# Delaying the recurrence scan by one more head, squaring in place, and one temporary fewer in the quantiser, in an eight-core layer kernel

## The reference, cut to what matters

```
# recurrent branch, h = 32 heads, n = 128 states
delta = softplus(delta_bias[..., :, None] + B_ssm[..., None, :])
hst   = exp(d_t * A) * hst + d_t * d_t          # over 2048 steps
y     = einsum('blhn,bln->blh', hs, C_ssm)
s     = ((y[..., None] + xg * Dp) * sigmoid(xn @ Wg + bg)) @ Wo
# feed-forward branch, twice: quantise the activations, take the sign of the weights
x_q = clip(round(x_norm * scale), -128, 127) / scale
w_q = sign(w) * mean(abs(w))
h   = gelu(x_q @ w1_q.T + b1);  f = quant(h) @ w2_q.T + b2
```

## Time and profile before

| | us |
|---|---|
| device time of the runs of this kernel | 3325.84 and 3452.18, median 3389.01 |
| profiled execution | 3321.91 |
| its span, slowest core (core 5) | 3320.1 |
| spans of the eight cores | 3305.1 to 3320.1, granted TensorE clock 0.766 to 0.768 |
| VectorE busy | 1435.8 (43% of the span) |
| TensorE matmuls busy | 1668.6 (50%) |
| ScalarE busy | 928.3 (28%) |
| GpSimd busy | 620.7 (19%) |

### The profile page before, as it was taken

The page is one execution under the profiler, slowest core; times in us unless marked ns, Lnnn a source line. Parts: engine busy times, 40 slices in busy tenths (PEclk is TensorE's granted clock), DMA queues, the critical chain, the costliest instruction groups (busy, mean ns, idle before and its releaser), DMA issues.

```text
span 3320.1 us, 23086 instructions; the slowest of 8 cores (3305.1 to 3320.1 us)
## 1 busy us (share of the span) xinstructions
PE 1668.6 (50%) x6432; PEld 648.1 (20%) x6432; DVE 1435.8 (43%) x1415; ACT 928.3 (28%) x981; POOL 620.7 (19%) x264
## 2 busy tenths in 40 slices
PE   2221263434342383777777777760000039999942
PEld 1100120000000131333332332320000014444421
DVE  4566334444544131222222222228999913333355
ACT  3100025545453010000222222221111155464322
POOL 0000013333333000000333333324444400000000
PEclk9999975555555796888888888875555569999965
DMA  4100125555553506111222222223333364554244
GB/s 116 51 26 26 18 42 123 107 121 111 117 115 88 90 1 101 38 38 64 102 102 102 102 102 102 101 77 116 123 115 123 108 215 175 178 203 177 77 152 165
DMA packets 129723, 340.84 MB, mean 103 GB/s; under 512 B 17664, under 2 KB 68992, under 8 KB 114080
## 3 DMA queue, kind: packets, MB, share of 16 engines
q1 hardware_dynamic: 114144, 287.78, 24.8%
q0 software_dynamic: 15456, 51.58, 10.1%
HBM read 290.10 MB, written 100.66 MB: 118 GB/s over the span
## 4 chain that ended last, share of the span: by engine, by line
PE 42%; DVE 22%; issue 12%; ACT 8%; DMA 7%; POOL 4%; another core or an unknown queue 3%; DVEq 1%; SPq 0%; ACTq 0%; POOLq 0%
PE pmA L816 15%; PE pmA L1012 14%; DVE p_t L952 6%; PE pmA L731 4%; DMA p_s<-s1Tsc 4%; POOL p_u L626 3%; PE pmA L695 3%; DVE p_t L945 2%; DVE aw L608 2%; ACT p_dmp L603 2%; ACT p_w L612 2%; PE pmC L401 2%; ACT p_d L621 2%; DVE p_k L949 1%
## 5 line engine op out<-in xcount | busy, mean ns | idle before, releaser
L1012 PE MATMUL pmA<-p_k2g,p_s 128*128 128x512 bf16 x2048 | 460.9, 382 | 474.2 <-ACT p_s L1001 474.2
L816 PE MATMUL pmA<-k1T,p_s 128*128 128x512 bf16 x2048 | 484.2, 396 | 168.3 <-DMA p_s<-s1Tsc 168.3
L1012 PEld LDWEIGHTS pmA<-p_k2g,p_s 128*128 128x128 bf16 x2048 | 191.8, 98 | 744.3 <-issue 535.9
L841 POOL TENSOR_TENSOR p_acs<-p_acs,p_h 128x1024 f32<-128x1024 f32 x63 | 213.2, 3383 | 432.0 <-ACT p_h L831 432.0
L581 PE MATMUL pmA<-ehl,bsel_t 32*128 32x512 bf16 x256 | 108.7, 562 | 365.5 <-DVE p_d L588 354.9
L816 PEld LDWEIGHTS pmA<-k1T,p_s 128*128 128x128 bf16 x2048 | 199.1, 101 | 454.4 <-issue 259.0
L824 DVE TENSOR_TENSOR p_h<-pmA,p_a1b 128x512 f32<-128x512 f32 x128 | 88.5, 691 | 380.6 <-PE pmA L816 380.3
L1026 DVE TENSOR_TENSOR p_S<-p_S,pmA 128x1024 f32<-128x1024 f32 x112 | 136.7, 1221 | 260.6 <-PE pmA L1012 260.6
L548 DVE TENSOR_TENSOR_SCAN p_h<-p_a,p_u 128x2048 f32<-128x2048 f32 x32 | 141.6, 4424 | 236.5 <-POOL p_u L626 236.5
L939 POOL TENSOR_TENSOR p_v<-p_hg,p_c2b 128x1024 f32<-128x1024 f32 x64 | 177.4, 2773 | 263.2 <-ACT p_int L942 233.6
L827 ACT ACTIVATE p_hg<-p_h,p_b1c 128x512 f32<-128x512 f32 x128 | 92.4, 722 | 458.2 <-DVE p_h L824 458.2
(11 more groups left out here) (160 smaller groups left out, 1806.8 us busy)
## 6 DMA issues: line engine op xcount, KB each, us to landing
p_w<-w2T SPq DMA_DIRECT2D x64, 1024.0 KB, 5.1
p_w<-w1T POOLq DMA_DIRECT2D x64, 512.0 KB, 10.4
s1Tsc<-p_w SPq DMA_DIRECT2D x256, 128.0 KB, 7.2
p_s<-s1Tsc SPq DMA_DIRECT2D x16, 2048.0 KB, 8.7
hgsc<-p_hg SPq DMA_DIRECT2D x64, 512.0 KB, 2.6
p_hg<-hgsc SPq DMA_DIRECT2D x64, 512.0 KB, 3.5
p_xb<-x_sh SPq DMA_DIRECT2D x16, 1024.0 KB, 5.8
k2Tsc<-p_k SPq DMA_DIRECT2D x64, 256.0 KB, 2.1
```

What stands on the lines that cost most here:

```text
L816: bld.op(TE, lambda e, k=k, icl=icl, tc=tc, pb=pb, sb_=sb_: e.matmul(pb[:, 0:512], sb_[:, k * 512 + icl * 128:k * 512 + (icl + 1) * 128], ...
L841: bld.op(GP, lambda e, h2b=h2b: e.tensor_add(acs[:], acs[:], h2b[:]), reads=[(h2b, 0), (h2b, 1), (acs, 0)], writes=[(acs, 0)])
L1012: bld.op(TE, lambda e, ic=ic, ds=ds, tc=tc, pb=pb, kg=kg, s2b=s2b: e.matmul(pb[:, tc * 512:(tc + 1) * 512], s2b[:, ic * 2048 + ds * 128:ic ...
```

## The change

In the recurrence:

- The scan and its product with C (`tail_vg`) for head h-1 are no longer called in iteration h; both `tail_vg` and `tail_y` are now called for head h-2, one behind the other. The last two heads follow after the loop.
- The square is written over `p_d` itself, the tile `p_u` is gone, and the scan reads `p_d`. `p_d` and `p_a` have three buffers instead of two. Since ScalarE's L623 (exp) reads `p_d`, the square now waits for it, and no longer only for L621 (ln).
- ScalarE's absolute sum of an odd w1 tile is done in two halves of 1024 columns, each with its own column of `aw1`, which grows to 128 columns; a memset clears its second half and the final sum reads 128 columns. The scratch tile that takes the unused output shrinks from 2048 to 1024 columns.

In the quantiser loop the first comparison is written into `p7_v` (float32) instead of `p7_k2` (bf16).

```
-        d_t = [ctx.enter_context(nc.sbuf_tensor(f"p4_d{i}", [128, T], F32)) for i in range(2)]
-        a_t = [ctx.enter_context(nc.sbuf_tensor(f"p4_a{i}", [128, T], F32)) for i in range(2)]
-        u_t = [ctx.enter_context(nc.sbuf_tensor("p4_u0", [128, T], F32))] * 2
+        d_t = [ctx.enter_context(nc.sbuf_tensor(f"p4_d{i}", [128, T], F32)) for i in range(3)]
+        a_t = [ctx.enter_context(nc.sbuf_tensor(f"p4_a{i}", [128, T], F32)) for i in range(3)]
...
-            at_, ut_, ht_, ypt = a_t[h % 2], u_t[h % 2], h_t[h % 2], yp_t[h % 2]
+            at_, ut_, ht_, ypt = a_t[h % 3], d_t[h % 3], h_t[h % 2], yp_t[h % 2]
...
-            if h > 0:
-                tail_vg(h - 1)
             if h > 1:
+                tail_vg(h - 2)
                 tail_y(h - 2)
...
-                    bld.op(SC, lambda e, wb=wb, q=q, aw1_=aw1_: e.activation(
-                        out=s1dmp[:], in_=wb[:], func=AF.Abs,
-                        accum_out=aw1_[:, q:q + 1]),
-                        reads=[(wb, 0)], writes=[s1dmp, (aw1_, f"a1_{q}")])
+                    for hf in range(2):
+                        bld.op(SC, lambda e, wb=wb, q=q, hf=hf, aw1_=aw1_: e.activation(
+                            out=s1dmp[:], in_=wb[:, hf * 1024:(hf + 1) * 1024], func=AF.Abs,
+                            accum_out=aw1_[:, 64 * hf + q:64 * hf + q + 1]),
+                            reads=[(wb, 0)], writes=[s1dmp, (aw1_, f"a1_{64 * hf + q}")])
...
-            bld.op(GP, lambda e, dt_=dt_, ut_=ut_: e.tensor_mul(
-                ut_[:], dt_[:], dt_[:]),
-                   reads=[(dt_, 0), (dt_, 1)], writes=[ut_])
+            bld.op(GP, lambda e, dt_=dt_: e.tensor_mul(
+                dt_[:], dt_[:], dt_[:]),
+                   reads=[(dt_, 0), (dt_, 1)], writes=[(dt_, 0), (dt_, 1)])
+        tail_vg(H - 2)
+        tail_y(H - 2)
         tail_vg(H - 1)
-        tail_y(H - 2)
         tail_y(H - 1)
...
-    bld.op(VE, lambda e: e.reduce_sum(out=alphas[:, 80:81], in_=aw1[:, 0:64], axis=AX.X),
+    bld.op(VE, lambda e: e.reduce_sum(out=alphas[:, 80:81], in_=aw1[:, 0:128], axis=AX.X),
...
-                bld.op(VE, lambda e, tb=tb, k2c=k2c: e.tensor_scalar(
-                    out=k2c[:], in0=tb[:], scalar1=-256.5, scalar2=None, op0=ALU.is_gt),
-                    reads=[(tb, 0)], writes=[(k2c, 0)])
+                bld.op(VE, lambda e, tb=tb, vb=vb: e.tensor_scalar(
+                    out=vb[:], in0=tb[:], scalar1=-256.5, scalar2=None, op0=ALU.is_gt),
+                    reads=[(tb, 0)], writes=[(vb, 0)])
```

More of the change, by code:

```diff
@@ L195, in build_program @@
         a1col = sb("a1col", [128, 24], F32)
-        aw1 = sb("aw1", [128, 64], F32)
+        aw1 = sb("aw1", [128, 128], F32)
         epsc = sb("epsc_t", [128, 8], F32)
@@ L247, in build_program @@
                                 for i in range(4)]
-                        s1dmp = s45.enter_context(nc.sbuf_tensor("p45_dmp", [128, 2048], BF16))
+                        s1dmp = s45.enter_context(nc.sbuf_tensor("p45_dmp", [128, 1024], BF16))
                         env.update(w1sl=w1sl, s1dmp=s1dmp)
@@ L550, in tail_vg @@
                 initial=0.0, op0=ALU.mult, op1=ALU.add),
-                   reads=[at_, ut_], writes=[ht_])
+                   reads=[at_, (ut_, 0), (ut_, 1)], writes=[ht_])
             bld.op(GP, lambda e, ht_=ht_, ypt=ypt: e.tensor_mul(
@@ L571, in w1_load @@
                 writes=[(wb, 0)], slot=f'w1e{q % 4}')
+        bld.op(VE, lambda e: e.memset(L["aw1"][:, 64:128], 0.0),
+               writes=[(L["aw1"], "zz")])
         for q in range(2):
@@ L575, in _p4 @@
         for h in range(H):
-            dt_, at_, ut_ = d_t[h % 2], a_t[h % 2], u_t[h % 2]
+            dt_, at_ = d_t[h % 3], a_t[h % 3]
             for half in (0, 1):
@@ L650, in _p45 @@
     pmB = L["pmB"]
-    ard = [(aw1, f"a1_{oc}") for oc in range(64)]
-    bld.op(VE, lambda e: e.reduce_sum(out=alphas[:, 80:81], in_=aw1[:, 0:64], axis=AX.X),
+    ard = ([(aw1, f"a1_{oc}") for oc in range(64)]
+           + [(aw1, f"a1_{64 + oc}") for oc in range(1, 64, 2)] + [(aw1, "zz")])
+    bld.op(VE, lambda e: e.reduce_sum(out=alphas[:, 80:81], in_=aw1[:, 0:128], axis=AX.X),
            reads=ard, writes=[(alphas, "rs1")])
@@ L948, in _p6 @@
                     reads=[(vb, 0), (intb, 0)], writes=[(tb, 0)])
-                bld.op(VE, lambda e, tb=tb, k2c=k2c: e.tensor_scalar(
-                    out=k2c[:], in0=tb[:], scalar1=-256.5, scalar2=None, op0=ALU.is_gt),
-                    reads=[(tb, 0)], writes=[(k2c, 0)])
-                bld.op(VE, lambda e, tb=tb, k2c=k2c: e.scalar_tensor_tensor(
-                    out=tb[:], in0=tb[:], scalar=-255.5, in1=k2c[:],
+                bld.op(VE, lambda e, tb=tb, vb=vb: e.tensor_scalar(
+                    out=vb[:], in0=tb[:], scalar1=-256.5, scalar2=None, op0=ALU.is_gt),
+                    reads=[(tb, 0)], writes=[(vb, 0)])
+                bld.op(VE, lambda e, tb=tb, vb=vb: e.scalar_tensor_tensor(
+                    out=tb[:], in0=tb[:], scalar=-255.5, in1=vb[:],
                     op0=ALU.is_gt, op1=ALU.add),
-                    reads=[(tb, 0), (k2c, 0)], writes=[(tb, 0)])
+                    reads=[(tb, 0), (vb, 0)], writes=[(tb, 0)])
                 bld.op(VE, lambda e, tb=tb, intb=intb, k2c=k2c: e.scalar_tensor_tensor(
```

## The result

The changed kernel is slower by 1.5%: the ratio to the kernel before is 1.015, with a 95% interval of 1.0134 to 1.0166. Over ten executions the kernel before has a median of 3326.34 us, so the 3389.01 us shown ahead of the prediction, of two executions, was high; 1.015 times 3326 is 3376 us, beside a forecast of 3377. The median of all eleven executions of the changed kernel is 3385.85 us. The forecast was added up from the profiled execution, and against that it says 1.7% slower. Set against the 3389 that was shown, the same 3377 says 0.4% faster, which is the wrong way.

What follows compares the result with a forecast made beforehand. The recurrence was taken as a chain of waits, the scan waiting for GpSimd's square, with VectorE busiest in the quantiser loop. Forecast: 3321.9 + 43 (recurrence) + 12 (quantiser) + 0.5 (memset and sum) = 3377 us, range 3300 to 3402.

Steps and rivals of the forecast that it cites:

- The base of the sum: Whole kernel: the terms were added to the profiled execution, 3321.9 us, arguing against the shown median of 3389.
- The ring that opens, and the one that closes: Recurrence: lag two undoes the square-to-scan tie; the product in TensorE's queue holds up the next groups, scan ready at 17.21 us.
- wrong altogether: Recurrence: sign that would refute the prediction, an iteration under 17 us, or w1 loads that end a wait.
- The port blocks the scan as well: Recurrence: scan and GpSimd's square take turns on the port; scan mean near 7.7 us, 4.42 plus 3.26 blocked.
- The third rival: Recurrence: the scan does not block, every iteration 17.21 us, total 3295, or 3253 with a faster clock; chance 0.10.
- The two distances: Recurrence, from a scan's start: square starts at 16.99 us, next scan ready at 17.21, so the iteration costs 20.45.
- How often the scan wins: Recurrence: the scan reaches the port before the square in 2 of 27 repeated iterations, giving back 7 to 8 us.
- +43 us: Recurrence's whole term: 617.2 us from first to last scan against 566.7, +50, less 7 to 8 for two wins.
- The second distance: Recurrence: the second scan-to-scan distance in the sum, put at 17.2 us.
- The quantiser: Quantiser loop: GpSimd's multiplication is released later and gets the port first; 0.20 us more a tile, +12 us over 62 tiles.
- The first: Recurrence: scan and square take turns, iterations of 17.2 and 20.5 us alternate, say +4 us, total 3338; chance 0.25.
- The second: Recurrence and quantiser: hand-overs cost more, x = 0.54, no win, quantiser at its upper end, total 3406 us; chance 0.13.

Runs made afterwards that it cites:

- Experiment 3: Changed kernel with the quantiser put back and TensorE's product issued one head later (h-3); 0.9492 of the kernel before, 169 us faster.
- experiment 6: Changed kernel, quantiser put back, absolute sum in one piece and two p_a buffers; 1.0022 of the kernel before, 7 us above it.
- experiment 2: Changed kernel with the quantiser put back, so the recurrence's part alone; 1.0108 of the kernel before, 36 us slower.
- experiment 5: Changed kernel, quantiser put back, absolute sum of an odd w1 tile in four quarters; 1.0037 of the kernel before, 12 us slower.
- experiment 4: Changed kernel, quantiser put back, square in its own tile, two buffers each for p_u, p_d, p_a; 0.9968 of the kernel before, 11 us faster.
- experiment 7: Experiment 3 with six w1 buffers, loads one iteration earlier and one scan output buffer; 0.9379 of the kernel before, 207 us faster.

## Which steps of the prediction failed, and which held

**The base of the sum.** This step failed. The sum starts from one profiled execution, 3321.9 us, and was not carried over to the median that was shown, 3389.01. Against that median 3377 us is 0.4% faster; the kernel is 1.5% slower. Ten executions of the kernel before bear the base itself out, with a median of 3326.34 us; above that base the working has 1.7% more, beside 1.5% measured. That 3377 lies 1 us from 1.015 times 3326 is in part luck: the base is 4 us under that median, and the recurrence's term is 7 to 9 us too large, as shown below.

**The ring that opens, and the one that closes.** Right. The square's wait vanished, and L558 standing behind the product in TensorE's queue is the new wait. Experiment 3 takes only that away and the iteration falls from 20.4 to 12.5 us. The prediction called an iteration under 17 us "wrong altogether", since TensorE's chain forbids it at the low clock; the distances of 15.8 to 16.5 us are of iterations in which TensorE was at the higher clock for part of that chain, as shown below.

**The port blocks the scan as well.** Right: 7.58 us for a scan with 0.29 us of delay behind a square. The rule in the Trainium skill, page "SBUF — State Buffer", section "SBUF: two separate sides", agrees with what the runs show for the scan, in both directions: 7.58 instead of 4.42 us, and a square of 6.82 instead of 3.59. The third rival, an unblocked scan, needed a square of 3.59 us beside a scan of 4.42; on no core do two such overlap by more than the 0.2 us of a hand-over.

**The two distances.** 16.99 and 17.21 us were forecast for square and scan, 20.45 for the iteration. Measured in the iteration above, the square stands at 20.09 from the nominal start of a scan that was itself blocked by 3.16 (7.58 - 4.42), so at 16.93; the scan 0.29 us behind it; the iteration is 20.38. The step that adds the halved sum, x = 0.40, is borne out by experiment 6, whose blocked iterations are 0.4 us shorter.

**How often the scan wins.** This step failed in its size, and it is the term of the +43 us that was mis-sized. I took two wins in the 27 repeated iterations, 7 to 8 us in all. There are two to five on a core, four in the middle, each 3.9 to 4.6 us shorter and not 3.25, which makes some 17 us. In every won iteration, on all cores, one or both of TensorE's groups took 1.1 to 1.6 us instead of 1.86, and most often more of them ran at the higher clock than the one group that I had counted: on core 3 both groups of a won iteration, 1.34 and 1.11 us at a granted clock of 0.82 and 0.95, beside 1.88 and 1.86 us at 0.50 on core 0. The argument against more wins, that the clock is back down in the iteration behind a win, does not hold either: on core 3, in the lost iteration between two wins, the second group took 1.11 us at a granted clock of 1.00. The second distance, forecast at 17.2, is 15.8 us on three cores and 20.4 on five. From the first scan's end to the last's the recurrence takes 590 to 603 us, 598 in the middle, where the sum had 614.7 less 7 to 8: 9 us too much.

The delay of the first scan, put at 2.5 us, held. On four cores of each trace the first w1 sum does not wait for its load, and there the first scan starts 21.5 us after TensorE's first group before, and 24.0 now. The term of 43 us was therefore 34 (598.1 - 566.7 + 2.5), beside 36 from experiment 2.

**The quantiser.** The size is right to 1 us (12 forecast, 13 measured), the order at the port behind it was not, so this agreement is luck. The prediction's own sign, L948 at 3.4 us, did not come: it takes 1.21, and L959 takes 3.39. I let the multiplication be released 0.27 us after its last reader and so get the port behind L956 (now L959). It is released 0.14 us after it (2430.40 + 1.23 to 2431.77) and is 0.03 us ahead of L959, which then stretches to 3.39 us. The 0.27 had been read off L945's end, though the row's own bracket named ScalarE's L942 as what released it. The tile is longer for another reason than I gave: before, the multiplication was already queued while L949 ran and took over the port within it (L939 ends at 2408.18, so its 2.34 us began at 2405.84, 0.25 before L952); now it has to be woken first and is only 0.03 ahead. The 0.22 us between the two is the 0.20 of the tile. This is read from the rows; no experiment moved it alone.

**The rivals.** The first, with scan and square taking turns, came to pass in experiment 5, and in part in experiment 6. The second, 3406 us, would have needed no wins and dearer hand-overs; there was neither.

## What to carry to other kernels

When a wait is cut by running one step further ahead, list every queue in which the moved result's consumer stands ahead of other work: here the fix of VectorE's wait put TensorE's queue in its place, and moving the consumer by one more step gave 5.1% instead of a loss. Where two engines share a port, two long operations that come to it 0.2 us apart are worth working out in both orders, because the loser drags its whole ring; a median duration that has grown in the profile is then the wait that the list of waits no longer shows. And an in-place write is not free if it moves the release from one reader to the next: it cost 47 us here.

## What the runs showed of the hardware that I had not expected

- Giving an engine more to do made the kernel 24 us faster (experiment 5 against 2), with no instruction removed.
- A square or a scan is delayed by what is left of the other, less a hand-over that is always the same: 3.16 us on the scan and 3.23 on the square (6.82 - 3.59) in the rows above. Over every such pair that overlaps by more than 0.2 us, on all cores of the changed kernel and experiments 2, 4, 5 and 6, the scan's delay is 0.13 to 0.15 us less than what was left of the square, and the square's 0.19 to 0.21 less than what was left of the scan.
- With the collisions gone (experiment 7) all eight cores alternate between 11.0 and 12.0 us, and take 356.4 to 356.6 us from the first scan to the last; in the changed kernel cores that run the same program differ by 13 us over the recurrence (590.1 to 602.8 us). It is not the collision as such: in experiment 4 the third to the thirtieth scan are blocked too, but always behind the square, and the cores agree to 1.4 us (551.5 to 552.9).
